# Attention and mixture-of-experts layer on one core: front with the norm in halves, loads in another order, fourth chunk's projections behind the first scores

## Chip, cores and metric

The kernel runs on one core of a Trainium2 chip. The metric is the device time in microseconds of one execution. Before the change three runs gave 443.89 to 449.31, with a median of 449.29.

## Reference

One layer: pre-norm attention with 16 heads of 8 columns, rotary position and a bias by relative distance, then a mixture of 8 experts (top 2 of 8, capacity 512) with a fallback for tokens that found no place. x has 2 batches of 1024 tokens of 128 columns.

```python
h = layernorm(x)
q, k, v = heads(h @ Wq + bq), heads(h @ Wk + bk), heads(h @ Wv + bv)
q = q * cos + rotate_half(q) * sin
k = k * cos + rotate_half(k) * sin
att = (einsum('bhid,bhjd->bhij', q, k) + bias[None]) * (1.0 / sqrt(D))
att = softmax(where(causal, att, -inf))
x = x + merge(einsum('bhij,bhjd->bhid', att, v)) @ Wp + bp
x = x + ffn(layernorm(x))       # router, top 2, experts, fallback
```

## The kernel before

The 2048 tokens are 16 tiles of 128 rows, handled as four chunks (c = 0 to 3) of four tiles; chunks 0 and 1 are batch 0. The 32 pairs of batch and head form 8 groups (n = 0 to 7) of four heads. One list, PLAN, holds all steps in order; each engine walks it and takes the steps that are its own, so the order of an engine's instructions is the order of the list. PROLOGUE is its beginning, called the front here:

- LN: VectorE's statistics of x (L1275, L1279), the reciprocal roots by three Newton steps, and xn_bias (L1283). XN c: the normalised tiles of chunk c (chunk 0 on VectorE, L1288, the others on ScalarE, L836). XT c: TensorE transposes them (L985), ScalarE copies them out (L844).
- VEC and ZERO: VectorE finishes the two vectors of relative-position factors and bias (L1294 to L1297), from which SP writes g_vec and r_vec, and clears ps_av (L1333).
- PROJ c i: q (i = 0) or k (i = 1) of chunk c, four passes of 512 columns (L997, L998), and VectorE's rotation (L1308, L1310, for chunks 0 and 1 also the sum L1317). For chunks 2 and 3 the sum is ADD, on GpSimd (L696).
- HI, REST, MID, LO c i: q and k are split into three bf16 parts: ScalarE rounds (HI, L853), GpSimd subtracts (REST, L702), ScalarE rounds (MID, L863), GpSimd subtracts (LO, L706). Then SP stores the parts (L527) and loads them into q_stack and k_stack in another layout (L565, L572, L575); half_in[0] and half_in[1] count the loads of chunks 0 and 1.
- LOAD: ScalarE issues the loads of b_all and f_all, tables of the other twelve heads, from r_vec and g_vec (L502). SP loads those of the first four heads.

Behind it follow, interleaved by the tables S_BEFORE and M_BEFORE: S n su, a score unit of group n for the row maxima (matmuls L1020 and L1024, VectorE's reduction L1346); M n h, the maxima of half h, turned and written to max_rows (L1152, L1354, L1356), which SP puts into q_stack (L591); ST, a transposed score (L1099), which for the first unit of a half waits for that put, and its exponential on ScalarE (L910); GpSimd's near product (L729, L732); AV (L1128). S, M and PROJ share two PSUM slots in turn, so a step's matmuls wait until VectorE has read the step two places earlier. FLIP turns f_all on TensorE (L1107). VP projects the values (L1004).

keep_warm runs matmuls whose result nobody reads (L964): WARM_FIRST of them before the bias vectors (L971, L975), WARM_PROJ after. GpSimd clears rows of the stacks first, waits for w_in (all four weights), and issues six small DMAs (L682 to L687).

## Time and profile before

| | |
|---|---|
| three runs | 449.29, 449.31, 443.89 us |
| profiled execution, its own time | 449.1 us |
| its span in the profile | 447.6 us |
| TensorE matmul busy | 383.8 us, 86% |
| VectorE busy | 309.2 us, 69% |
| ScalarE busy | 223.9 us, 50% |
| GpSimd busy | 268.4 us, 60% |

Times are from the start of the span. A row of a timeline has the start and the length of an instruction (or of several merged ones, with their number), and in brackets how long its engine was idle before it and who ended that. PE is TensorE, DVE is VectorE, ACT is ScalarE, POOL is GpSimd; SPq and ACTq are the queues from which SP and ScalarE issue DMAs. The granted clock is 1.00 at 2.4 GHz and 0.50 at 1.2 GHz.

### The profile page before, as it was taken

What the parts mean: (1) busy time and instruction counts of PE and PEld (TensorE: products, weight loads), DVE (VectorE), ACT (ScalarE), POOL (GpSimd) and SP (SyncE); (2) the same over time, 40 slices, a digit from 0 to 9 for tenths busy, and PEclk for the clock granted to TensorE, in tenths of its full rate; (3) what the DMA queues carried; (4) which work ended last, traced back from release to release, by engine and by line L of the source; (5) the groups of instructions that cost most, each with busy time, mean ns of one, the idle gap of its engine ahead of it and who ended that gap; (6) DMA issues with size and microseconds to landing.
All of it is one profiled execution on the core that took longest, in us unless ns stands there. A gap on an engine that the chain in (4) does not pass through costs nothing.

```text
span 447.6 us, 7356 instructions
## 1 busy us (share of the span) xinstructions
PE 383.8 (86%) x2470; PEld 177.6 (40%) x2470; DVE 309.2 (69%) x722; ACT 223.9 (50%) x498; POOL 268.4 (60%) x242
## 2 busy tenths in 40 slices
PE   8885788999999999999989989997878677999810
PEld 2432434444434334444435334432334325566500
DVE  3786787866777876877875998875366548566514
ACT  1650245767666776666677755767741110333200
POOL 7375084578569778558589358779712460166650
PEclk9998999999999999999999999999985678999965
DMA  8596574203705008906005000004600102133118
GB/s 217 113 269 155 104 153 79 34 1 80 174 1 101 11 0 185 292 17 109 2 1 103 8 2 9 14 8 130 213 15 13 36 29 57 52 95 95 47 46 277
DMA packets 30459, 37.45 MB, mean 84 GB/s; under 512 B 4757, under 2 KB 25045, under 8 KB 30101
## 3 DMA queue, kind: packets, MB, share of 16 engines
q1 hardware_dynamic: 24378, 29.91, 27.8%
q0 software_dynamic: 2240, 4.21, 3.1%
q10 hardware_dynamic: 3808, 2.92, 2.3%
q8 instruction: 18, 0.29, 0.3%
q14 instruction: 15, 0.12, 0.1%
HBM read 28.56 MB, written 12.75 MB: 92 GB/s over the span
## 4 chain that ended last, share of the span: by engine, by line
PE 62%; DVE 18%; DMA 5%; POOL 5%; ACT 4%; issue 4%; SPq 1%; DVEq 0%; POOLq 0%; ACTq 0%
PE ps_av L1128 15%; PE ps_st L1099 12%; PE ps_slot L1020 12%; DVE neg_max L1346 7%; PE ps_slot L1024 5%; PE ps_st L1203 3%; PE ps_slot L1213 3%; ACT probs L910 2%; PE ps_slot L1159 2%; POOL probs L732 2%; DMA x_sb<-in_L_attn_x_dram 2%; PE ps_st L1205 2%; PE ps_st L1107 2%; PE ps_av L1205 1%; PE ps_st L1041 1%
## 5 line engine op out<-in xcount | busy, mean ns | idle before, releaser
L910 ACT ACTIVATE probs<-ps_st 128x512 f32<-128x512 f32 (+3 forms) x384 | 168.7, 494 | 102.0 <-PE ps_st L1099 99.8
L1346 DVE TENSOR_REDUCE neg_max<-ps_slot 128x1 f32<-128x640 f32 (+7 forms) x184 | 175.6, 989 | 55.0 <-PE ps_slot L1024 52.9
L732 POOL TENSOR_TENSOR probs<-probs,f_all 128x960 f32<-128x960 f32 (+2 forms) x65 | 123.8, 1904 | 10.3 <-ACT probs L910 5.5
L1020 PE MATMUL ps_slot<-k_stack,q_stack 128*128 128x512 bf16 (+3 forms) x384 | 99.5, 329 | 11.3 <-DVE neg_max L1346 6.3
L1099 PE MATMUL ps_st<-q_stack,k_stack 128*128 128x512 bf16 (+3 forms) x384 | 103.1, 329 | 2.8 <-ACT probs L910 2.5
L1128 PE MATMUL ps_av<-probs,v_all 128*9 128x512 f32 (+3 forms) x768 | 81.2, 497 | 2.1 <-POOL probs L732 1.6
L729 POOL TENSOR_SCALAR_AFFINE_SELECT probs<-probs 128x512 f32<-128x512 f32 x58 | 37.0, 638 | 68.7 <-ACT probs L910 68.5
L1024 PE MATMUL ps_slot<-b_all,flip_b 128*128 128x240 bf16 (+2 forms) x288 | 65.4, 252 | 0.0
L1099 PEld LDWEIGHTS ps_st<-q_stack,k_stack 128*128 128x128 bf16 x384 | 34.5, 97 | 74.0 <-ACT probs L910 54.0
L1020 PEld LDWEIGHTS ps_slot<-k_stack,q_stack 128*128 128x128 bf16 x384 | 35.8, 98 | 44.7 <-DVE neg_max L1346 13.1
L737 POOL DMA_INDIRECT slots<-token_rows,slot_no x32 | 33.2, 1039 | 32.3 <-DVEq L1534 24.4
L800 POOL DMA_INDIRECT parts<-probs,e_tok x32 | 31.1, 972 | 31.7 <-DVE probs L1661 23.3
L1024 PEld LDWEIGHTS ps_slot<-b_all,flip_b 128*128 128x128 bf16 x288 | 28.4, 99 | 13.9 <-issue 0.3
L1128 PEld LDWEIGHTS ps_av<-probs,v_all 128*9 128x9 f32 x768 | 11.7, 89 | 25.3 <-issue 18.0
L936 ACT ACTIVATE y_raw<-ps_st 128x512 f32<-128x512 f32 x16 | 9.6, 597 | 23.7 <-PE ps_st L1205 12.9
L1203 PE MATMUL ps_st<-probs 128*128 128x512 f32 x32 | 17.4, 626 | 2.0 <-DVE probs L1623 2.0
L1213 PEld LDWEIGHTS ps_slot<-k_stack,probs 128*128 128x128 f32 x128 | 14.9, 191 | 6.5 <-issue 3.7
L1213 PE MATMUL ps_slot<-k_stack,probs 128*128 (+1 forms) x128 | 16.0, 278 | 1.4 <-DVE probs L1650 1.4
L702 POOL TENSOR_TENSOR token_rows<-token_rows,part_all 128x512 f32<-128x512 f32 x6 | 7.4, 1229 | 13.9 <-ACT part_all L853 13.9
L1159 PE MATMUL ps_slot<-wide,y_raw 128*128 128x128 f32 x64 | 10.7, 292 | 3.8 <-DVE neg_max L1346 3.1
L964 PE MATMUL ps_st<-part_all,ones_b 128*128 128x512 bf16 x34 | 11.6, 444 | 1.6 <-POOL part_all L673 1.6
L930 ACT ACTIVATE probs<-ps_slot 128x512 f32<-128x512 f32 x8 | 4.8, 596 | 16.0 <-PE ps_slot L1195 16.0
(188 smaller groups left out, 403.5 us busy)
## 6 DMA issues: line engine op xcount, KB each, us to landing
q_stack<-q_parts SPq DMA_DIRECT2D x21, 192.0 KB
slots<-in_c_rows_dram SPq DMA_DIRECT2D x4, 528.0 KB, 9.3
probs<-slots SPq DMA_DIRECT2D x8, 264.0 KB, 2.7
parts<-in_c_rows_dram SPq DMA_DIRECT2D x4, 512.0 KB, 9.4
q_stack<-parts SPq DMA_DIRECT2D x4, 512.0 KB, 5.5
k_stack<-k_parts SPq DMA_DIRECT2D x14, 128.0 KB
f_all<-g_vec ACTq DMA_DIRECT2D x1, 1536.0 KB, 11.3
q_parts<-part_all SPq DMA_DIRECT2D x16, 96.0 KB, 3.3
```

Source lines behind the costliest of these rows:

```text
L729: pool.affine_select(out=diag, in_=diag, compare_op=ALU.is_ge, fill=0.0, base=0, pattern=[[0, HG], [1, P]], channel_multiplier=-1).then_in ...
L732: pool.tensor_tensor(pr, pr, f_of[:, n % (H // HG), :, fo:fo + hi - lo], ALU.mult).then_inc(near_done, 1)
L737: pool.indirect_dma_start(slots[:, :], bass.IndirectOffsetOnAxis(ap=slot_no[:, k, t:t + 1], axis=0), u_rows[:, t, :], None, bounds_check=E ...
L800: pool.indirect_dma_start(parts[:, :], bass.IndirectOffsetOnAxis(ap=e_tok[:, i, j:j + 1], axis=0), e_out[i][:, j, :], None, bounds_check=2 ...
L910: act.activation(probs[:, u % PBUF, g, c0:512], ps_st[:, ST_NO[what] % 3, c0:512], ACT.Exp, scale=SCALE).then_inc(exp_done, 1)
L1020: pe.matmul(ps_slot[:, slot, o + lo:o + hi], q_stack[:, buf, t // MT, g, t % MT * P:(t % MT + 1) * P], k_stack[:, buf, lo // CW, g, 0:hi - ...
L1024: mm = pe.matmul(ps_slot[:, slot, o + nlo:o + nhi], flip_b[:, :], b_of[:, n % (H // HG), g, f0:f0 + nhi - nlo], start=False, stop=True)
L1099: pe.matmul(ps_st[:, i % 3, c0:512], k_stack[:, n % NBUF, kt // CH, g, kt % CH * P:(kt % CH + 1) * P], q_stack[:, n % NBUF, qb, g, c0:512] ...
L1128: mm = pe.matmul(ps_av[32 * g:32 * g + VW, c0:512], v_all[:, n, kt, g, :], probs[:, u % PBUF, g, c0:512], start=(u in (0, CH)), stop=(u in ...
L1203: pe.matmul(ps_st[:, c, :], wgu[i][:, c * P:(c + 1) * P], slotT[i], start=True, stop=True)
L1213: mm = pe.matmul(ps_slot[:, 1, i * 512 + j * C:i * 512 + (j + 1) * C], gated[i][:, c, j * P:(j + 1) * P], wd_all[:, bass.ds(2 * e + c, 1), ...
L1346: dve.tensor_reduce(neg_max[:, t // MT, heads[0]:heads[-1] + 1, t % MT], src, AX.X, ALU.max, negate=True).then_inc(slot_used, 1)
```

## The change

LN comes in two halves of eight tiles. The first is whole on VectorE. Of the second, VectorE does the statistics and the first guess of the roots; the three Newton steps and the bias are late_roots on GpSimd, and XN 2 and XN 3, now in pieces of two tiles, wait for it. On SP's queue Wq and Wk stand behind x part 0, the rotary table comes in two halves, and Wv and Wp stand last; the four weights have two semaphores. LOAD waits for half_in[0] too and stands at the end of the front. The first heads' f_all is loaded after the first stacks. The first warming has 16 matmuls, not 24, the second 8, not 10. The steps of chunks 0 and 1 are interleaved in another way, and PROJ and ADD of chunk 3 stand between S 0 6 and M 0 0.

```diff
-WARM_FIRST, WARM_PROJ, WARM_SLOTS = 24, 10, 8
+WARM_FIRST, WARM_PROJ, WARM_SLOTS = 16, 8, 8
...
-    [0, 0, 0, 0, 0, 0, 0, 0, 0, 0, 0, 0, 0, 1, 1, 3, 7, 10, 13, 13, 16, 16, 16],
+    [0, 0, 0, 0, 0, 0, 0, 0, 0, 0, 0, 0, 1, 1, 3, 6, 9, 13, 13, 16, 16, 16, 16],
...
+LAST_CHUNK = [("PROJ", 3, 0), ("PROJ", 3, 1), ("ADD", 3, 0), ("ADD", 3, 1)]
...
             out.append((S_BEFORE[n][su], ("S", n, su)))
+            if (n, su) == (0, M_AT[0]):
+                out += [(0, item) for item in LAST_CHUNK]
...
+            load_x(0)
+            sp.dma_start(w_attn[:, 0, :], Wq[:, :]).then_inc(wqk_in, 16)
+            sp.dma_start(w_attn[:, 1, :], Wk[:, :]).then_inc(wqk_in, 16)
+            load_x(1)
+            load_turns(0)
+            load_x(2)
+            load_x(3)
+            load_turns(1)
+            for i, w in enumerate((Wv, Wp)):
+                sp.dma_start(w_attn[:, 2 + i, :], w[:, :]).then_inc(w_in, 16)
...
-            load_tiles(sp, f_all, g_vec, 0, HG, factors_in)
...
                 load_k(0, 0, (c,), half_in[c])
+            load_tiles(sp, f_all, g_vec, 0, HG, factors_in)
...
-            pool.wait_ge(w_in, 64)
+            pool.wait_ge(w_in, 32)
...
+            def late_roots():
+
+                r = slice(TPB, TT)
+                v, t, dst = newton[:, 0, r], newton[:, 1, r], rstd[:, 0, r]
+                pool.wait_ge(late_guess, 1)
+                for _ in range(3):
+                    after(pool.tensor_tensor(t, dst, dst, ALU.mult))
+                    after(pool.tensor_tensor(t, t, v, ALU.mult))
+                    after(pool.tensor_scalar(t, t, -0.5, 1.5, ALU.mult, ALU.add))
+                    after(pool.tensor_tensor(dst, dst, t, ALU.mult))
+                after(pool.tensor_tensor(xn_bias[:, r], mv[:, r, 0], dst, ALU.mult))
+                after(pool.tensor_scalar(xn_bias[:, r], xn_bias[:, r], -1.0, None, ALU.mult))
+                pool.sem_inc(late_bias, 1)
...
-            act.wait_ge(w_in, 64)
+            act.wait_ge(wqk_in, 32)
...
                     act.wait_ge(vec_out, 32)
+                    act.wait_ge(half_in[0], HALF_IN)
                     load_tiles(act, b_all, r_vec, HG, H - HG, toep_rest)
...
+                if h:
+                    root_guess(rstd[:, 0, r], newton[:, 0, r])
+                    dve.sem_inc(late_guess, 1)
+                else:
+                    rsqrt(rstd[:, 0, r], newton[:, 0, r], newton[:, 1, r])
+                    dve.scalar_tensor_tensor(out=xn_bias[:, r], in0=mv[:, r, 0], scalar=-1.0, in1=rstd[:, 0, r],
+                                             op0=ALU.mult, op1=ALU.mult).then_inc(bias_done, 1)
```

GpSimd's queue in the front, before: the last two of the six DMAs, then REST (L702) and LO (L706) of chunk 0.

```order
L686 DMA fw<-in_L0_ffn_fWu_dram 128x64
L687 DMA fw<-in_L0_ffn_fWd_dram 64x128
L702 ISA
L702 TENSOR_TENSOR token_rows<-token_rows,part_all 128x512 [waits part_hi] x2
L706 TENSOR_TENSOR part_all<-token_rows,part_all 128x512 [waits part_mid] x2
L702 TENSOR_TENSOR token_rows<-token_rows,part_all 128x512 [waits part_lo,part_hi] x2
L706 TENSOR_TENSOR part_all<-token_rows,part_all 128x512 [waits part_mid] x2
```

The same place after. L774 to L779 are late_roots, of whose 14 instructions the last six stand here; REST is L722, LO is L726.

```order
L774 TENSOR_TENSOR newton<-rstd 128x8 [waits own_pool]
L775 TENSOR_TENSOR newton<-newton 128x8 [waits own_pool]
L776 TENSOR_SCALAR newton<-newton 128x8 [waits own_pool]
L777 TENSOR_TENSOR rstd<-rstd,newton 128x8 [waits own_pool]
L778 TENSOR_TENSOR xn_bias<-mv,rstd 128x8 [waits own_pool]
L779 TENSOR_SCALAR xn_bias<-xn_bias 128x8 [waits own_pool]
L722 TENSOR_TENSOR token_rows<-token_rows,part_all 128x512 [waits own_pool,part_hi]
L726 TENSOR_TENSOR part_all<-token_rows,part_all 128x512 [waits part_mid]
L722 TENSOR_TENSOR token_rows<-token_rows,part_all 128x512 [waits part_hi]
L726 TENSOR_TENSOR part_all<-token_rows,part_all 128x512 [waits part_mid]
L722 TENSOR_TENSOR token_rows<-token_rows,part_all 128x512 [waits part_lo,part_hi] x2
L726 TENSOR_TENSOR part_all<-token_rows,part_all 128x512 [waits part_mid] x2
```

The 14 instructions stand between the six DMAs and REST 0 0, and LO 0 0 now stands before REST 0 1.

VectorE's queue at the first score units, before: the end of chunk 3's rotations (L1308, L1310), seven reductions of S (L1346), and the first M (L1354, L1356).

```order
L1308 SCALAR_TENSOR_TENSOR probs<-ps_slot,bcol_perm,wide 128x512 [waits rope_half,slot_full]
L1310 SCALAR_TENSOR_TENSOR probs<-ps_slot,bcol_perm,wide 128x512
L1308 SCALAR_TENSOR_TENSOR probs<-ps_slot,bcol_perm,wide 128x512 [waits rope_half,slot_full]
L1310 SCALAR_TENSOR_TENSOR probs<-ps_slot,bcol_perm,wide 128x512
L1346 TENSOR_REDUCE neg_max<-ps_slot 128x4 [waits rope_half,slot_full]
L1346 TENSOR_REDUCE neg_max<-ps_slot 128x2 [waits slot_full] x6
L1354 CAST max_rows<-ps_slot 16x128 [waits slot_full]
L1356 TENSOR_TENSOR max_rows<-ps_slot,max_rows 16x128 [waits mrows_sb0]
```

After: rotation L1364 and L1366, reduction L1404, M L1412 and L1414.

```order
L1404 TENSOR_REDUCE neg_max<-ps_slot 128x4 [waits rope_half,slot_full]
L1404 TENSOR_REDUCE neg_max<-ps_slot 128x2 [waits slot_full] x6
L1364 SCALAR_TENSOR_TENSOR probs<-ps_slot,bcol_perm,wide 128x512 [waits slot_full]
L1366 SCALAR_TENSOR_TENSOR probs<-ps_slot,bcol_perm,wide 128x512
L1364 SCALAR_TENSOR_TENSOR probs<-ps_slot,bcol_perm,wide 128x512 [waits rope_half,slot_full]
L1366 SCALAR_TENSOR_TENSOR probs<-ps_slot,bcol_perm,wide 128x512
L1412 CAST max_rows<-ps_slot 16x128 [waits rope_half,slot_full]
L1414 TENSOR_TENSOR max_rows<-ps_slot,max_rows 16x128 [waits mrows_sb0]
```

The four instructions of chunk 3's rotations now stand between the seven reductions and the first M.

SP's queue from the store of r_vec to the first stack loads, before:

```order
L547 DMA r_vec<-y_raw 16x384 [waits vec_done]
L547 DMA g_vec<-y_raw 16x384
L502 DMA b_all<-r_vec 128x4x256 [waits vec_out]
L502 DMA f_all<-g_vec 128x4x256
L527 DMA q_parts<-part_all 32x3x512 [waits part_lo]
L527 DMA k_parts<-part_all 32x3x512 [waits part_lo]
L565 DMA q_stack<-q_parts 24x2048 [waits first_out0]
```

And after:

```order
L567 DMA r_vec<-y_raw 16x384 [waits vec_done]
L567 DMA g_vec<-y_raw 16x384
L509 DMA b_all<-r_vec 128x4x256 [waits vec_out]
L547 DMA q_parts<-part_all 32x3x512 [waits part_lo]
L547 DMA k_parts<-part_all 32x3x512 [waits part_lo]
L584 DMA q_stack<-q_parts 24x2048 [waits first_out0]
```

The load of f_all is gone from this place; it stands behind the stack loads of both halves.

## Rows read from the trace of the kernel before

**Rows 1.** Stretches: busy time per engine, granted clock (PEclk), DMA share, GB/s

```profile
40.00:41.00 1.00, 1.00 (x6) 0.63 (x5) 0.43 (x2) 0.00 (x0) 0.00 (x0) 0.50 0.60 184
...
80.00:90.00 10.00, 10.00 (x70) 4.43 (x69) 8.12 (x11) 8.12 (x17) 6.86 (x6) 1.00 0.09 17
```

**Rows 2.** Chain of waits, 0 to 80 us: start, length, what

```profile
27.59 4.97 DMA q_parts<-part_all
...
35.23 2.94 DMA k_stack<-k_parts
...
71.86 0.39 PE ps_st L1099
```

**Rows 3.** Timeline of VectorE: start, length, line, what, idle before

```profile
7.14 1.82 DVE L1275 BATCH_NORM_STATS2 stats<-x_sb 128x6 f32<-128x128 f32 x8 [0.64 <-DMA x_sb<-in_L_attn_x_dram]
...
10.01 0.87 DVE L1275 BATCH_NORM_STATS2 stats<-x_sb 128x6 f32<-128x128 f32 x4 [1.04 <-DMA x_sb<-in_L_attn_x_dram]
...
10.91 1.17 DVE L1279 BATCH_NORM_AGGREGATE mv<-stats 128x2 f32<-128x6 f32 x16
...
14.76 0.17 DVE L1283 SCALAR_TENSOR_TENSOR xn_bias<-mv,rstd 128x16 f32<-128x16 f32 x1
...
15.88 0.54 DVE L1294 TENSOR_TENSOR y_raw<-y_raw,y_all 16x384 f32<-16x384 f32 x1
...
17.13 0.48 DVE L1333 MEMSET ps_av<- 128x512 f32 x1 [0.18 <-DVE bcol_perm L1297]
...
19.38 0.75 DVE L1308 SCALAR_TENSOR_TENSOR token_rows<-ps_slot,bcol_perm,wide 128x512 f32<-128x512 f32 x1 [1.76 <-PE ps_slot L998]
```

**Rows 4.** Timeline of TensorE, warming and bias vectors

```profile
1.59 9.37 PE L964 MATMUL ps_st<-part_all,ones_b 128*128 128x512 bf16 x24 [1.59 <-POOL part_all L673]
...
10.89 1.46 PE L971 MATMUL ps_slot<-y_all,tab 32*16 32x384 f32 x4
...
12.75 2.32 PE L964 MATMUL ps_st<-part_all,ones_b 128*128 128x512 bf16 x10
```

**Rows 5.** Timeline of GpSimd in the front

```profile
11.30 0.74 POOL L682 DMA_DIRECT2D router<-in_L_ffn_Wr_dram  x1 [2.08 <-DMA w_attn<-in_L_attn_Wp_dram]
...
14.59 0.54 POOL L687 DMA_DIRECT2D fw<-in_L_ffn_fWd_dram  x1
...
22.39 1.15 POOL L702 TENSOR_TENSOR token_rows<-token_rows,part_all 128x512 f32<-128x512 f32 x1 [7.26 <-ACT part_all L853]
...
25.95 2.72 POOL L706 TENSOR_TENSOR part_all<-token_rows,part_all 128x512 bf16<-128x512 f32 x2
```

**Rows 6.** Timeline of GpSimd, roots of the second norm, first and last

```profile
223.45 0.22 POOL L753 TENSOR_TENSOR newton<-rstd 128x16 f32<-128x16 f32 x1 [0.66 <-DVEq L1417]
...
227.31 0.24 POOL L760 TENSOR_SCALAR xn_bias<-xn_bias 128x8 f32<-128x8 f32 x1
```

**Rows 7.** Timeline of ScalarE in the front

```profile
21.68 0.63 ACT L853 ACTIVATE part_all<-token_rows 128x512 bf16<-128x512 f32 x1 [1.26 <-DVE token_rows L1317]
...
24.66 1.63 ACT L836 ACTIVATE probs<-x_sb,xn_bias,rstd 128x128 f32<-128x128 f32 x4
```

**Rows 8.** Line L519's issue, then DMA issues with us to landing

```profile
L519 SPq DMA_DIRECT2D wide<-in_c_wide_dram x1: 432/432/432, 5.7 to 5.7; - x1
...
f_all<-g_vec ACTq DMA_DIRECT2D x1, 1536.0 KB, 11.3
...
wide<-in_c_wide_dram SPq DMA_DIRECT2D x1, 1024.0 KB, 9.1
...
r_vec<-y_raw SPq DMA_DIRECT2D x1, 12.0 KB, 2.0
```

**Rows 9.** Timeline of VectorE, last rotations and first maximum

```profile
32.74 0.75 DVE L1308 SCALAR_TENSOR_TENSOR probs<-ps_slot,bcol_perm,wide 128x512 f32<-128x512 f32 x1 [0.64 <-PE ps_slot L998]
...
34.46 0.75 DVE L1308 SCALAR_TENSOR_TENSOR probs<-ps_slot,bcol_perm,wide 128x512 f32<-128x512 f32 x1 [0.31 <-PE ps_slot L998]
...
46.44 0.28 DVE L1354 CAST max_rows<-ps_slot 16x128 bf16<-16x128 f32 x1 [0.37 <-PE ps_slot L1152]
```

More of the change, by code:

```diff
@@ L382, in layer_kernel @@
         t_in = sem("t_in")
-        rope_in = sem("rope_in")
+        rope_in = [sem(f"rope_in{h}") for h in range(2)]
+        bv_in = sem("bv_in")
         ones_in = sem("ones_in")
@@ L831, in _, with normalise @@
             act.activation(below_b[:, :], below, ACT.Copy).then_inc(const_b, 1)
[L833 to L835 removed]
+            def normalise(c, tiles):
+                for t in tiles:
+                    if c < 2:
+                        act.wait_ge(bias_done, 1)
+                    else:
+                        act.wait_ge(late_bias, 1)
                     act.activation(xn[c][:, t % CH, :], x_sb[:, t, :], ACT.Identity, bias=xn_bias[:, t:t + 1],
@@ L872, in _ @@
                 if kind == "XN":
-                    if what[1]:
-                        normalise(what[1])
+                    c = what[1]
+                    if c == 1:
+                        normalise(c, range(CH, 2 * CH))
+                    elif c:
+                        first = c * CH + what[2] * CH // 2
+                        normalise(c, range(first, first + CH // 2))
                 elif kind == "XT":
@@ L1269, in _, with first_norm @@
             stat_count = [0]
-            def first_norm():
-                for t in range(TT):
+            def first_norm(h):
+                tiles = range(h * TPB, (h + 1) * TPB)
+                for t in tiles:
                     if t % CH == 0:
```

57 lines of the change are left out of this document (32 added, 25 removed).

## Prediction

> **What bounds the kernel now.** I read the chain of waits first, then the timeline of 0 to 80 us, the stretches with the granted clock, and the DMA landings. After 80 us TensorE is busy all the time (10.00 of 10 us in the stretch 80:90, VectorE 8.12 [rows 1]), and the diff changes nothing there. So the change can only move the moment from which TensorE runs without gaps. That moment is the first transposed score of group 0's second half, at 71.86 [rows 2].
>
> Ahead of it stand two chains. The first is the front: x lands in four parts, the last statistics start at 10.01, the bias is there at 14.76 + 0.17, the first rotation starts at 19.38 [rows 3]; its split runs through ScalarE and GpSimd, the q part is stored at 27.59 (4.97 us to land), and the last k_stack load (issued 35.23, 2.94 us) lands at 38.17 [rows 2]. Only then does the first score unit run. The second is group 0's maxima on VectorE: seven units, then M at 46.44 [rows 9], and on to 71.86. VectorE has nothing to do in the last 3 us before 38.2: its last rotation starts at 34.46 and takes 1.4 us [rows 9]. A task that now lies in those 3 us is free.
>
> **The norm in halves.** x part 1 now queues behind Wq and Wk (640 KB instead of 512 KB up to its end). Before, it landed at 7.14 and part 3 at 10.01 [rows 3]; I take 8.0. Four statistics 0.87 (8.9), eight aggregates at 1.17/16 = 0.07 us each (9.5), the chain to the bias (14.76 - 12.08 = 2.7) gives 12.2, the first normalise 1.1 gives 13.3. Then VectorE does the second half before the vectors: eight statistics 1.8, eight aggregates 0.6, three steps of the guess 0.6: 16.3. VEC and ZERO took from 15.88 to 17.61 [rows 3], 1.7 us, so the first rotation can start at 18.0. TensorE's side: 24 warming matmuls took 9.37, so 16 end near 7.8; the bias vectors' matmul started at 10.89 [rows 4] at the latest when its inputs were there; 1.86 us more to the second warming, which is now 8 x 0.23 = 1.9. So TensorE is free for x at 14.65 or earlier; transpose, copy and projection took from 15.9 (normalise done, VEC starts) to 19.38, 3.5 us, which gives 18.1 at most. VectorE and TensorE are level: rotation at **18.0 instead of 19.38, 1.4 us earlier**, its sum at 20.3.
>
> **What GpSimd now has in its queue.** Each of its three steps must be passed by REST(0,0). First, it waits for w_in before six DMAs; these took 11.30 to 15.13 [rows 5]. Wv and Wp were ahead of the rotary table, and are now behind it: the bytes on SP's queue up to their end are those up to the table's end before (x, four weights, 1024 KB), and that landed at 5.75 + 9.1 = 14.85 [rows 8]. So the six DMAs run from about 15.2 to 19.0. Second, the roots: 14 small instructions, each waiting for the one before. The same 14 stand in the trace later, from 223.45 to 227.55 [rows 6]: 4.1 us, giving 23.1. Third, REST(0,0), which started at 22.39 before [rows 5]; HI(0,0) would have been ready for it at 20.3 + 0.63 = 20.9. So it starts at **23.1, 0.7 later than before**, and the 1.4 us won on VectorE are not seen. If the weights landed where they did before (11.3), the roots would end at 16.3 + 4.1 = 20.4 and REST would start at 21.0; if at 16.5, at 24.7. I take 14.85, the equal byte count.
>
> From there: REST 1.15 (24.3), MID 0.63 (24.9), HI(0,1) (25.6), REST(0,1) behind LO(0,0) 26.2 to 27.4. In between ScalarE has four tiles of the late norm (1.63 [rows 7]) and a copy like HI's 0.6: MID(0,1) 27.9 to 28.5, LO(0,1) 1.2: the k part is stored at 29.7 (28.70 before).
>
> **The tables later.** ScalarE's 2304 KB for the other heads, which took 11.3 us to land [rows 8], lay over the first stores and loads. Now they wait for half_in[0]. A store with free DMA engines landed in 2.0 (r_vec [rows 8]) against 4.97. So k lands at 31.8; four issues of 0.37 follow, the last load takes between 2.0 and 2.94: first score unit at 35.3 to 36.2, I take 35.8, **2.4 earlier** than 38.2. With the bounds on the weights above it is 33.4 to 37.4. What the tables now lie over: loads for the second half (needed about 12 us later), and the put of the first maxima. 2304 KB and some 1.6 MB on SP's queue from 36 on end by about 48, when the first maxima go out. I count nothing, up to 3 us if that put is late. The first four heads' factors are issued at about 40 and needed at 51: nothing.
>
> At this place the trace gives GpSimd beside VectorE: two L706 in 2.72, 1.36 each, against 1.15 for an L702 [rows 5]. The Trainium skill (SBUF — State Buffer, Who interferes with whom) says more: a GpSimd instruction and a VectorE one with two SBUF inputs exclude each other for their whole duration. By that rule the two sums of rotations at 19 to 23 would put up to 1.4 us on the roots and the time at 451.8. The row doesn't ask for that much, so I leave it out.
>
> **The fourth chunk's projections.** They leave the 3 us in which VectorE waited and go between unit 6 and M(0,0), where VectorE is the chain. A rotation waits for its projection, and two in a row started 34.46 - 32.74 = 1.72 apart [rows 9]. The slot for the first comes free at the end of unit 5; the projection takes 1.72 and some 0.3 until VectorE sees it, less a unit's 1.1 on VectorE (seven from 38.2 to 46.07): 0.9 idle. Then 1.7 and 1.5 for the second: 4.1, less the 0.37 for which M waited before [rows 9]: **3.75 us more**. Between 3.0 (the bare work) and 4.2 (nothing saved). The scores' order in group 0 is put back by one unit: one more after the first AV, one fewer before it; I count zero. The two ADDs on GpSimd (two of about 1.2, as L702) end before its first near product. The new waits for bv_in and w_in stand at the values' projection, after 50 us, and both transfers have landed by 17; ScalarE's copies of Wq and Wk start earlier than before and nobody waits for them.
>
> **Sum.** 449.1 (profiled run) - 2.4 + 3.75 = **450.4**, against a median of 449.29 that the profiled run matches within 0.2. Bounds: -4.8 + 3.0 gives 447.3, -0.8 + 4.2 gives 452.5. A measurement of this kernel tells 2% (9 us) from no change, not this.
>
> **Rivals.** (a) The later gaps of VectorE take up part of the 3.75, or GpSimd is not in the way: first unit at 33.8, 1.5 us added: 446.2. For it: VectorE does wait for TensorE now and then after 46 us. Against: it is the queue in front of TensorE's gaps there. (b) **Slower:** TensorE's clock falls in the new gap. Warming ends at 7.8 and the next matmul waits until 10.1 to 10.9, up to 3.1 us. In the trace TensorE stood from 34.4 to 38.2 and the granted clock was 0.50, 1.2 GHz, at 40:41 [rows 1]. If it falls here, the bias vectors, eight warming matmuls, transposes and first projection take double: 1.9 + 1.9 for the first two and some 2.4 of the 3.5 us more, 5.7 to 6.2 in all, which puts the rotation's sum at 26 and REST(0,0) at 26.6, 3.5 past the 23.1: up to 453.9, half of that if the clock comes back on the way. It decides once the gap is long enough for the clock; shorter gaps than 3.8 us bring no fall in the trace. The Trainium skill (TensorE: Matmul & The Clock Gate, HAM oscillation) says the same of a DMA wait: the next matmuls run at half rate. By that rule this rival holds if this gap is long enough, which no row shows. (c) The late put of the first maxima, 3 us on top: 453.4. (d) The three runs of before spread from 443.89 to 449.31; if the changed kernel's median is of the lower kind, it is 450.4 - 5.4 = 445. (e) The norm in halves does nothing, because x part 1 lands only at 10: rotation at 20.0, still ahead of GpSimd's 23.1, so 450.4 again.
>
> **Chances.** Forecast with (e) 0.55, time 450.4, own range 447.3 to 452.5. (a) 0.15, (b) and (c) 0.13 together, (d) 0.17. The range takes in (d) and (b): 444.5 to 453.8. No case reaches 2% (440.3 or 458.3): same 0.96, 0.02 on each side.
>
> **What the profile would show.** GpSimd's REST(0,0) starting right behind the roots near 23; Wv and Wp landing near 15; k's store landing in about 2 us; first score unit near 35.8; two rotations and some 4 us between unit 6 and M(0,0) at about 47.8; the first transposed score of the second half near 73. Wrong if GpSimd is free by 21, if the clock row of 10 to 14 reads 0.5, or if VectorE's added 3.75 is not found again at 72.

## The result and the profile after

The changed kernel is **slower, by 2.0%**: a median of 456.95 us in four runs (454.50 to 459.26) against 449.06 in four runs of the kernel before, a ratio of 1.0203 with a 95% interval of 1.0109 to 1.0296. So the loss is clear of the noise, and whether it reaches 2% is open. The forecast was 450.4, with a range of 444.5 to 453.8. The profiled execution took 459.26 with a span of 457.2, the longest of its four; before it was 449.1 with 447.6. So the two profiles differ by 10.2 us and the medians by 7.9.

From the first maxima behind 100 us on, the two traces run side by side: the maxima's cast that stands at 103.75 before stands at 111.98 after, 8.2 later, and the last one, at 305.85, stands at 314.08, again 8.2 later. So the time is lost before 80 us. The chain of waits of the changed kernel (start, length, what) names the transfers that end last:

```profile
7.18 9.14 DMA w_attn<-in_L_attn_Wp_dram
...
31.53 1.82 DMA k_parts<-part_all
...
35.15 2.74 DMA q_parts<-part_all
...
43.52 9.13 DMA k_parts<-part_all
...
57.35 9.31 DMA k_parts<-part_all
...
67.93 0.23 PE ps_st L1146
```

The first row is the wait for Wv and Wp. The next two are stores of chunk 0 and of chunk 1 for the first four heads. The last two DMA rows are the stores of group 1 and of groups 2 and 3. Before, the chain had the 4.97 us of q_parts at 27.59 and then none of these stores [rows 2].

**Front.** GpSimd's timeline, the answer to [rows 5] and [rows 6]: it waits 7.40 us for Wp, issues six DMAs, does the 14 small root instructions (L774 to L779), and only then REST 0 0 (L722), 2.62 later than the 22.39 of before:

```profile
16.62 0.74 POOL L702 DMA_DIRECT2D router<-in_L_ffn_Wr_dram  x1 [7.40 <-DMA w_attn<-in_L_attn_Wp_dram]
...
19.92 0.54 POOL L707 DMA_DIRECT2D fw<-in_L_ffn_fWd_dram  x1
20.57 0.21 POOL L774 TENSOR_TENSOR newton<-rstd 128x8 f32<-128x8 f32 x1
...
22.58 0.51 POOL L777 TENSOR_TENSOR rstd<-rstd,newton 128x8 f32<-128x8 f32 x1
...
24.59 0.24 POOL L779 TENSOR_SCALAR xn_bias<-xn_bias 128x8 f32<-128x8 f32 x1
25.01 1.15 POOL L722 TENSOR_TENSOR token_rows<-token_rows,part_all 128x512 f32<-128x512 f32 x1 [0.18 <-POOL xn_bias L779]
```

VectorE in the front and at the first maxima, the answer to [rows 3] and [rows 9]. The rotation starts at 18.39 instead of 19.38; between the last reduction and M stand chunk 3's two rotations, with 1.01 and 0.31 idle ahead of them, and M comes at 49.15 instead of 46.44:

```profile
8.32 0.87 DVE L1324 BATCH_NORM_STATS2 stats<-x_sb 128x6 f32<-128x128 f32 x4 [1.96 <-DMA x_sb<-in_L_attn_x_dram]
9.23 0.64 DVE L1328 BATCH_NORM_AGGREGATE mv<-stats 128x2 f32<-128x6 f32 x8
...
12.32 0.17 DVE L1337 SCALAR_TENSOR_TENSOR xn_bias<-mv,rstd 128x8 f32<-128x8 f32 x1
...
18.39 0.75 DVE L1364 SCALAR_TENSOR_TENSOR token_rows<-ps_slot,bcol_perm,wide 128x512 f32<-128x512 f32 x1
...
45.88 0.75 DVE L1364 SCALAR_TENSOR_TENSOR probs<-ps_slot,bcol_perm,wide 128x512 f32<-128x512 f32 x1 [1.01 <-PE ps_slot L1043]
...
47.60 0.75 DVE L1364 SCALAR_TENSOR_TENSOR probs<-ps_slot,bcol_perm,wide 128x512 f32<-128x512 f32 x1 [0.31 <-PE ps_slot L1043]
...
49.15 0.28 DVE L1412 CAST max_rows<-ps_slot 16x128 bf16<-16x128 f32 x1
```

TensorE, the answer to [rows 4] and further on. It has a gap of 1.96 ahead of the bias vectors; one of 3.84 in which it waits for the late norm (ScalarE's L876, which waits for the roots); the first score unit at 37.75; the wait for the put of the first maxima, their transfer into q_stack (1.12); and at 67.93 a wait of 2.36 for ScalarE. The first transposed score of the second half comes at 79.85, 71.86 before [rows 2]:

```profile
1.60 6.29 PE L1009 MATMUL ps_st<-part_all,ones_b 128*128 128x512 bf16 x16 [1.60 <-POOL part_all L693]
9.84 1.46 PE L1016 MATMUL ps_slot<-y_all,tab 32*16 32x384 f32 x4 [1.96 <-DMA y_all<-in_c_mask_dram]
...
12.04 3.20 PE L1009 MATMUL ps_st<-part_all,ones_b 128*128 128x512 bf16 x8
...
28.17 0.95 PE L1030 MATMUL ps_st<-wide,probs 128*128 128x128 f32 x4 [3.84 <-ACT probs L876]
29.81 2.07 PE L1042 MATMUL ps_slot<-acts,w_attn 128*128 128x512 f32 x2 [0.69 <-ACT acts L884]
...
37.75 0.23 PE L1067 MATMUL ps_slot<-k_stack,q_stack 128*128 128x128 bf16 x1 [1.15 <-DMA k_stack<-k_parts]
...
54.12 0.39 PE L1146 MATMUL ps_st<-q_stack,k_stack 128*128 128x512 bf16 x1 [1.12 <-DMA q_stack<-max_rows]
...
67.93 0.23 PE L1146 MATMUL ps_st<-q_stack,k_stack 128*128 128x128 bf16 x1 [2.36 <-ACT probs L955]
...
79.85 0.38 PE L1146 MATMUL ps_st<-q_stack,k_stack 128*128 128x512 bf16 x1
```

Why ScalarE was late at 67.93 is one row of its timeline. HI 2 0 writes part_all, which the stores of groups 2 and 3 still read, and the exponentials of the last units stand behind it:

```profile
67.08 0.63 ACT L893 ACTIVATE part_all<-y_raw 128x512 bf16<-128x512 f32 x1 [3.18 <-DMA k_parts<-part_all]
```

The same copy in the kernel before:

```profile
60.63 0.63 ACT L853 ACTIVATE part_all<-y_raw 128x512 bf16<-128x512 f32 x1 [0.29 <-DMA k_parts<-part_all]
```

The stretches (length, busy time of PE, PEld, DVE, ACT, POOL, granted clock, DMA share, GB/s) answer to [rows 1]. Behind each of the three gaps of TensorE (1.96, 3.84 and 2.36 us) the granted clock is down, to 0.66, 0.50 and 0.66, with 0.77 and 0.80 in the two stretches after the last; before, it was 1.00 in 66:70, 70:74 and 74:78.

```profile
10.00:14.00 4.00, 4.00 (x13) 1.71 (x12) 3.59 (x20) 0.48 (x1) 0.00 (x0) 0.66 1.19 266
...
30.00:34.00 4.00, 4.00 (x7) 1.83 (x8) 0.38 (x1) 2.70 (x6) 3.65 (x4) 0.50 0.28 76
...
66.00:70.00 4.00, 2.04 (x7) 0.92 (x8) 1.11 (x2) 0.96 (x3) 3.92 (x4) 0.92 0.64 113
70.00:74.00 4.00, 2.83 (x9) 0.78 (x8) 3.54 (x4) 1.97 (x5) 2.74 (x4) 0.66 0.13 20
...
80.00:90.00 10.00, 9.49 (x68) 4.33 (x69) 7.88 (x14) 6.61 (x13) 2.60 (x3) 1.00 0.63 89
```

The DMA issues of the first 80 us (queue, KB each, median us to landing) of the changed kernel:

```profile
f_all<-g_vec ACTq DMA_DIRECT2D x1, 1536.0 KB, 15.5
...
q_parts<-part_all SPq DMA_DIRECT2D x8, 96.0 KB, 5.4
k_parts<-part_all SPq DMA_DIRECT2D x8, 96.0 KB, 8.4
```

and of the kernel before:

```profile
q_parts<-part_all SPq DMA_DIRECT2D x8, 96.0 KB, 3.8
k_parts<-part_all SPq DMA_DIRECT2D x8, 96.0 KB, 4.7
```

So the 10.2 us between the profiled executions are: -0.46 up to the first score unit (38.21 to 37.75), +3.17 from there to M (8.23 to 11.40), **+5.28 from M to the second half's first transposed score** (25.42 to 30.70), +1.6 from there to the end of the span and +0.6 around it. Of the 5.28, 3.74 lie ahead of HI 2 0, which starts 17.93 behind M instead of 14.19. The other 1.54 lie behind it, where the granted clock is down.

### The profile page after: what moved, and what is told of

The parts are those of the page before. It is cut to its first block, busy times and chain, and to the rows that moved or that the text cites. A ratio compares the mean times of both kernels' runs of the same rounds, so it can differ in the third digit from the quotient of the medians.

```text
span 457.2 us, 7288 instructions
## 1 busy us (share of the span) xinstructions
PE 380.3 (83%) x2409; PEld 179.6 (39%) x2460; DVE 309.2 (68%) x725; ACT 224.1 (49%) x498; POOL 271.4 (59%) x256
## 4 chain that ended last, share of the span: by engine, by line
PE 57%; DVE 15%; DMA 8%; POOL 6%; issue 5%; ACT 4%; SPq 4%; DVEq 0%; POOLq 0%; ACTq 0%
PE ps_av L1175 14%; PE ps_st L1146 11%; PE ps_slot L1067 10%; DVE neg_max L1404 5%; DMA k_parts<-part_all 4%; PE ps_slot L1071 4%; ACT probs L955 4%; PE ps_st L1250 3%; PE ps_slot L1260 3%; DMA w_attn<-in_L_attn_Wp_dram 2%; PE ps_slot L1206 2%; PE ps_st L1252 2%; PE ps_av L1252 1%; PE ps_st L1088 1%; PE ps_st L1154 1%
## 5 line engine op out<-in xcount | busy, mean ns | idle before, releaser
L1404 DVE TENSOR_REDUCE neg_max<-ps_slot 128x1 f32<-128x640 f32 (+7 forms) x184 | 175.8, 989 | 56.8 <-PE ps_slot L1071 54.7
L1146 PE MATMUL ps_st<-q_stack,k_stack 128*128 128x512 bf16 (+3 forms) x369 | 99.7, 329 | 6.8 <-ACT probs L955 5.0
L1067 PE MATMUL ps_slot<-k_stack,q_stack 128*128 128x512 bf16 (+3 forms) x366 | 96.0, 330 | 9.6 <-DVE neg_max L1404 5.5
L757 POOL DMA_INDIRECT slots<-token_rows,slot_no x32 | 33.4, 1045 | 33.6 <-DVEq L1592 25.6
L726 POOL TENSOR_TENSOR part_all<-token_rows,part_all 128x512 bf16<-128x512 f32 x8 | 9.3, 1158 | 9.8 <-ACT part_all L903 9.8
L1438 DVE SCALAR_TENSOR_TENSOR probs<-probs,f_all 128x960 f32<-128x960 f32 (+2 forms) x7 | 8.5, 1213 | 5.8 <-ACT probs L955 5.8
## 6 DMA issues: line engine op xcount, KB each, us to landing
slots<-in_c_rows_dram SPq DMA_DIRECT2D x4, 528.0 KB, 10.2
```

Of the source, the lines that this page charges most:

```text
L757: pool.indirect_dma_start(slots[:, :], bass.IndirectOffsetOnAxis(ap=slot_no[:, k, t:t + 1], axis=0), u_rows[:, t, :], None, bounds_check=E ...
L1067: pe.matmul(ps_slot[:, slot, o + lo:o + hi], q_stack[:, buf, t // MT, g, t % MT * P:(t % MT + 1) * P], k_stack[:, buf, lo // CW, g, 0:hi - ...
L1146: pe.matmul(ps_st[:, i % 3, c0:512], k_stack[:, n % NBUF, kt // CH, g, kt % CH * P:(kt % CH + 1) * P], q_stack[:, n % NBUF, qb, g, c0:512] ...
L1404: dve.tensor_reduce(neg_max[:, t // MT, heads[0]:heads[-1] + 1, t % MT], src, AX.X, ALU.max, negate=True).then_inc(slot_used, 1)
```

## The experiments

Twelve kernels. The table has the starts in us that their traces show, in the order of the work, and their times. S is the first score unit, M the first maxima's cast, "second half" the first transposed score of it. The comparisons are with the kernel before on the same chip, for the changed kernel as for the others; HI 2 0 has its wait in brackets.

| kernel | REST 0 0 | S | M | HI 2 0 (waited) | second half | median | ratio, 95% |
|---|---|---|---|---|---|---|---|
| before | 22.39 | 38.21 | 46.44 | 60.63 (0.29) | 71.86 | 449.06 | |
| changed | 25.01 | 37.75 | 49.15 | 67.08 (3.18) | 79.85 | 456.95 | 1.0203 [1.0109, 1.0296] |
| a_tables | 26.24 | 38.91 | 50.31 | 64.77 (1.01) | 76.67 | 453.31 | 1.0101 [1.0046, 1.0156] |
| a_proj | 26.41 | 40.19 | 48.86 | 67.05 (0.67) | 79.22 | 457.47 | 1.0161 [1.0096, 1.0227] |
| a_warm | 25.31 | 37.96 | 49.35 | 66.23 (0.25) | 78.87 | 457.70 | 1.0180 [1.0125, 1.0234] |
| a_pool | 23.84 | 36.02 | 48.78 | 65.06 (1.81) | 76.86 | 460.61 | 1.0260 [1.0207, 1.0314] |
| a_pool2 | 22.88 | 35.30 | 47.96 | 64.55 (1.70) | 76.29 | 456.82 | 1.0159 [1.0100, 1.0217] |
| b_proj | 22.00 | 37.60 | 50.02 | 64.41 (0) | 76.47 | 453.52 | 1.0095 [1.0067, 1.0123] |
| b_tables | 21.82 | 34.52 | 42.36 | 64.90 (3.38) | 75.92 | 452.72 | 1.0072 [1.0034, 1.0109] |
| a_combo | 21.64 | 35.57 | 43.57 | 58.69 (1.67) | 70.61 | 448.58 | 0.9973 [0.9936, 1.0011] |
| a_sp | 24.93 | 37.20 | 48.60 | 62.15 (0) | 86.17 | 465.25 | 1.0385 [1.0330, 1.0440] |
| b_sp | 21.88 | 34.45 | 42.46 | 58.07 (1.71) | 82.25 | 458.15 | 1.0193 [1.0159, 1.0227] |
| c_best | 21.22 | 34.48 | 43.15 | 58.12 (0) | 81.31 | 459.85 | 1.0236 [1.0204, 1.0269] |
| c_split | 21.22 | 34.48 | 43.06 | 58.89 (0) | 71.92 | 448.97 | 0.9957 [0.9922, 0.9991] |

### One part undone in the changed kernel

**a_tables**: the other heads' tables where they were.

```diff
-            ("HI", 0, 0), ("REST", 0, 0), ("PROJ", 0, 1), ("XN", 2, 0), ("MID", 0, 0), ("HI", 0, 1), ("PROJ", 1, 0),
+            ("HI", 0, 0), ("REST", 0, 0), ("PROJ", 0, 1), ("LOAD",), ("XN", 2, 0), ("MID", 0, 0), ("HI", 0, 1), ("PROJ", 1, 0),
...
-            ("XT", 3), ("PROJ", 2, 1), ("LO", 1, 0), ("MID", 1, 1), ("LO", 1, 1), ("ADD", 2, 0), ("LOAD",), ("ADD", 2, 1)]
+            ("XT", 3), ("PROJ", 2, 1), ("LO", 1, 0), ("MID", 1, 1), ("LO", 1, 1), ("ADD", 2, 0), ("ADD", 2, 1)]
...
-                    act.wait_ge(half_in[0], HALF_IN)
```

> The changed kernel, with the other heads' tables loaded as before: ScalarE issues them behind HI 0 0, with no wait for half_in[0]. Theory T (the tables, in flight from 38 us, hold up the stores for the next group, so that the load of stack 1 is issued at 52.7 instead of 48.1, the stores behind it land at 66.7 and ScalarE's HI 2 0 waits 3.2 us for them): the first stores take about 5 us again and the first score unit is at 39 to 41, but the 3.2 us wait of HI 2 0 is gone, first maxima to first transposed score of the second half is back from 30.7 to about 26 us, and the time is 3 to 5 us under the changed kernel's (about 453). Rival P (the chunk 3 projections are the price): the distance from first maxima to that score stays at 30 and the time stays or rises by 2. Rival C (TensorE's clock in the front is the price): no fall of the time either.

The score units start 1.16 later, and yet the second half starts 3.2 earlier and the median is 3.6 lower. The distance from M to the second half falls from 30.70 to 26.36 (25.42 before). The late tables cost more behind the first scores than they give ahead of them. What is left, 453.31 against 449.21 of the kernel before beside it, is 4.1, the price that chunk 3's projections have alone (b_proj, below).

**a_proj**: chunk 3's projections back at the end of the front.

```diff
-            if (n, su) == (0, M_AT[0]):
-                out += [(0, item) for item in LAST_CHUNK]
...
-    out = list(PROLOGUE)
+    out = list(PROLOGUE) + LAST_CHUNK
```

> The changed kernel, with chunk 3's projections and sums back at the end of the front, ahead of the first score unit. My prediction's price for them behind unit 6 was 3.75 us on the first maxima. Theory P: first maxima 2.5 to 3.7 us earlier than 49.15 (with the first score unit 0 to 1 later, as VectorE rotates until about 41 there), time 2.5 to 3.7 lower. Theory T: the stores for the next group are still late behind the tables, so HI 2 0 waits longer by what the maxima win, and the time falls by under 1.5 us.

No change of the time. In this front the old place is not free either: chunk 2's rotations wait 3.33 us for TensorE, which waits for the late norm, so the scores start 2.44 later, and M only 0.3 earlier. HI 2 0 waits 0.67 for its stores and not longer, as the expectation had it, and still starts at 67.05; a_warm, the next run, shows the other way there. What the move costs had to be asked of the front of before (b_proj, below).

**a_warm**: WARM_FIRST and WARM_PROJ at 24 and 10 again.

```diff
-WARM_FIRST, WARM_PROJ, WARM_SLOTS = 16, 8, 8
+WARM_FIRST, WARM_PROJ, WARM_SLOTS = 24, 10, 8
```

> The changed kernel, with 24 and 10 warming matmuls as before. Theory C: the granted clock stays 1.00 from 10 to 14 us (0.66 in the changed kernel), first rotation at 17.9 to 18.1 instead of 18.39; if the clock were the cause of the loss the time would fall by 3 us or more. Theories T and P: GpSimd's roots end at 24.9 all the same and the time stays within 1 us.

The gap at 8 to 10 us is gone and the granted clock there is back at full, as the stretch shows:

```profile
10.00:14.00 4.00, 4.00 (x17) 1.53 (x17) 3.56 (x25) 0.48 (x1) 0.00 (x0) 1.00 1.16 277
```

The rotation starts at 18.78, no earlier than the 18.39 of the changed kernel, and the time is the same. The fall of the clock in the warming was there and cost nothing. The second fall, behind the wait for the norm, stands as in the changed kernel: 0.50 in 30:34.

One row of the table asks for more: HI 2 0 waits only 0.25 for its stores here, not 3.18, and yet the second half starts just 1.0 earlier. The stores are not the only way by which time is lost there. The put of the first maxima, beside the tables too, took from 50.35 to 54.45, and then TensorE ran at the lower clock, so that its four passes of FLIP took 3.41 us (1.88 in the changed kernel and before):

```profile
54.50 0.61 PE L1146 MATMUL ps_st<-q_stack,k_stack 128*128 128x512 bf16 x1 [0.58 <-DMA q_stack<-max_rows]
...
54.90 3.41 PE L1154 MATMUL ps_st<-f_all,wide 128*128 128x512 f32 x4
...
54.00:58.00 4.00, 3.50 (x5) 1.52 (x6) 0.91 (x1) 1.19 (x2) 0.00 (x0) 0.50 0.82 158
```

In a_proj it is the same: the put takes 5.06, TensorE waits 2.27 for it, and the four passes take 3.33. Before, the granted clock was 1.00 in 54:58. Whether the fall of the clock hangs on the tables is not shown.

**a_pool** and **a_pool2**: GpSimd's wait for w_in and the six DMAs later, in a_pool ahead of BP 0 (146 us), in a_pool2, whose edit stands here, at the first score unit.

```diff
-            pool.wait_ge(w_in, 32)
-            pool.dma_start(router[:, :], Wr[:, :]).then_inc(late_in, 16)
...
+            def late_loads():
+
+                pool.wait_ge(w_in, 32)
+                pool.dma_start(router[:, :], Wr[:, :]).then_inc(late_in, 16)
...
             for what in PLAN:
...
+                elif what == ("S", 0, 0):
+                    late_loads()
```

> The changed kernel, with GpSimd's wait for Wv and Wp and its six small DMAs moved out of the front to just before the output bias. The roots then start when VectorE's guess is there (16.4) and end near 20.5 instead of 24.9. If GpSimd's queue held the front: REST 0 0 at 21.4 instead of 25.0, XN 2 at 20.6, TensorE not idle for 3.8 us, k stored at 28 instead of 31.5, first score unit near 34.5 instead of 37.8, and the time about 3 us lower (454) if the delay is passed on. Theory T says that the wait of HI 2 0 for its stores stays, since tables and stores move together. Rival: if the front's gain is eaten by later waits on DMAs, the time stays.

> The changed kernel, with GpSimd's wait for w_in and its six DMAs at the first score unit, where GpSimd stood idle for 8 us in the changed kernel's trace. In the run before this one the same DMAs stood ahead of the output bias; the front was better by 3.0 us at the first transposed score of the second half (76.86 against 79.85), and 3.0 us were lost again where AV waited for GpSimd. Here: the same front, no such wait, time 3 us under the changed kernel's, 453.5 to 455. If the later loss was not these DMAs, it is seen again between 150 and 170 us and the time stays at 460.

With the loads out of the way the roots start at 17.02 instead of 20.57 in a_pool2 (GpSimd now waits for VectorE's guess, not for a weight), REST 0 0 comes 2.13 earlier and the score units 2.45:

```profile
17.02 0.20 POOL L767 TENSOR_TENSOR newton<-rstd 128x8 f32<-128x8 f32 x1 [7.80 <-DVEq L1339]
```

That shows who held the front. The profiled run was 454.5, but the median is 456.82, level with the changed kernel's 456.95 and above the 453.5 to 455 expected; four runs each don't tell how much of the 2.45 reaches the end. In a_pool the place was badly chosen. The six issues take 3.9 us of GpSimd at 146.30 to 150.18, where TensorE has no slack:

```profile
154.39 1.04 PE L1181 MATMUL ps_av<-probs,v_all 128*9 128x256 f32 x8 [2.96 <-POOL probs L745]
```

and the time rises to 460.61.

### One part alone in the kernel before

**b_proj**: only chunk 3's projections behind unit 6.

```diff
-            ("PROJ", 3, 0), ("PROJ", 3, 1), ("ADD", 2, 1), ("ADD", 3, 0), ("ADD", 3, 1)]
+            ("ADD", 2, 1)]
...
+LAST_CHUNK = [("PROJ", 3, 0), ("PROJ", 3, 1), ("ADD", 3, 0), ("ADD", 3, 1)]
...
+            if (n, su) == (0, M_AT[0]):
+                out += [(0, item) for item in LAST_CHUNK]
```

> The kernel before, with only chunk 3's projections and sums moved behind score unit 6 of group 0. My price: first maxima 3.75 us later (50.2), passed on in full, time 449.2 + 3.75 = 453. If later gaps of VectorE take it up: 450 or less. If the front's 3 us of VectorE idle ahead of the first unit were needed for other work, less than 3 us as well.

+4.1 us (453.52 against 449.38 of the kernel before beside it). VectorE's timeline has the pattern that the prediction worked out, 1.0 idle, a rotation, 0.3 idle, a rotation:

```profile
46.75 0.75 DVE L1312 SCALAR_TENSOR_TENSOR probs<-ps_slot,bcol_perm,wide 128x512 f32<-128x512 f32 x1 [1.01 <-PE ps_slot L1002]
...
48.47 0.75 DVE L1312 SCALAR_TENSOR_TENSOR probs<-ps_slot,bcol_perm,wide 128x512 f32<-128x512 f32 x1 [0.31 <-PE ps_slot L1002]
...
50.02 0.28 DVE L1358 CAST max_rows<-ps_slot 16x128 bf16<-16x128 f32 x1
```

From S to M it is 12.42 instead of 8.23, and the 4.2 are still there at the second half (+4.6) and at the end.

**b_tables**: only the tables later, behind half_in[0], and the first heads' f_all behind the stacks.

```diff
-            load_tiles(sp, f_all, g_vec, 0, HG, factors_in)
...
                 load_k(0, 0, (c,), half_in[c])
+            load_tiles(sp, f_all, g_vec, 0, HG, factors_in)
...
+                    act.wait_ge(half_in[0], HALF_IN)
```

and LOAD moved from behind PROJ 0 1 to ahead of the last ADD.

> The kernel before, with only the tables moved: the other heads' behind half_in[0], the first heads' f_all behind the stacks. Theory T: first stores land in about 2 us instead of 5, first score unit near 35 instead of 38.2, first maxima 3 us earlier; but the stores for the next group land about 9 us after their issue, the load of stack 1 is issued at 50 or later, HI 2 0 waits 2 us or more, and the first transposed score of the second half is not earlier than 71.9: time 449 to 453. Rival: if the stores are not held up, the 3 us stay and the time is 446.

The front gains 3.7 us (34.52 instead of 38.21), more than the 3.0 that the prediction gave the faster landing, and all of it is lost again, twice over: the second half starts 4.1 later and the median is 3.3 higher. The two stores in its chain of waits:

```profile
40.54 10.04 DMA k_parts<-part_all
...
55.27 9.21 DMA k_parts<-part_all
```

and the copy that waits for the second:

```profile
64.90 0.63 ACT L853 ACTIVATE part_all<-y_raw 128x512 bf16<-128x512 f32 x1 [3.38 <-DMA k_parts<-part_all]
```

That is the pattern of the changed kernel without any of its other edits. Stack 1 is loaded from 50.60 on, at 48.07 before, and M to second half takes 33.6 instead of 25.4. In between TensorE also stands for 3.28 us, up to 45.60, for the stack load of chunk 1, and its granted clock is 0.50 in 46:50; the changed kernel, whose M comes 6.8 later, has neither. So the two lose by the same stores, but not the same microseconds.

The traced execution took 447.88, the shortest of its ten, though its second half starts 4.1 later than before. It had the clock on its side at the end: 1.00 in 300:350 and 0.90 in 350:400, where the trace of before has 0.86 and 0.83. The start of the second half tells what the front costs; the time of one execution has the clock behind 300 us in it as well.

### The parts that are left, and better places

**a_combo**: the changed kernel with tables as before, GpSimd's loads as in a_pool2, warming 24 and 10, and chunk 3 in the front. What stays of the change: the norm in halves, SP's loads by need, the interleaved steps of chunks 0 and 1, the first heads' f_all behind the stacks. The edit is the diffs of a_tables, a_proj, a_warm and a_pool2 together.

> The changed kernel with four of its parts undone: tables issued behind HI 0 0 as before, GpSimd's six DMAs at the first score unit, 24 and 10 warming matmuls, chunk 3's projections back in the front. What remains is the norm in halves with the late roots on GpSimd, the loads in order of need, the interleaved front, and f_all of the first heads behind the stacks. Theory T with the roots' wait: the chain of the front is then the shorter one, first score unit near 36.5, first maxima near 45, first transposed score of the second half near 71, time 447 to 449, level with or just under the kernel before. If the halves are of no use in themselves (a late XN 2 lets TensorE's clock fall), 450 to 453.

448.58 in ten runs, level with before. The first score unit is 2.64 earlier, the second half 1.25 earlier. In the stretch 30:34 the clock is at 1.00, and the longest wait of TensorE for the norm there is 0.91, so the fall at this place went with that wait. The first heads' f_all behind the stacks stays in this kernel, so by itself it costs nothing that shows.

**a_sp**, **b_sp** and **c_best**: does the slow landing come from the tables, or are the stores slow by themselves? The tables are issued by SP behind the stores of groups 2 and 3, in the changed kernel, in the kernel before, and in the changed kernel with a_pool2's loads, full warming and chunk 3 in the front.

```diff
                 store_parts(c, (2, 3), parts_out[c])
+            load_tiles(sp, b_all, r_vec, HG, H - HG, toep_rest)
+            load_tiles(sp, f_all, g_vec, HG, H - HG, factors_rest)
...
-                    load_tiles(act, b_all, r_vec, HG, H - HG, toep_rest)
-                    load_tiles(act, f_all, g_vec, HG, H - HG, factors_rest)
```

> The changed kernel, but the two loads of the other heads' tables are issued by SyncE behind the stores of groups 2 and 3 (about 57 us), not by ScalarE behind half_in[0] (38 us). Theory (the tables, in flight from 38 to 53 us, hold up the stores of group 1, the put of the first maxima and the stores of groups 2 and 3): the stores of group 1 land in 4 us or less, stack 1 is loaded by 48, the put costs TensorE nothing, ScalarE's copy HI 2 0 waits under 1 us, and the first transposed score of the second half comes at 75 to 76.5 instead of 79.85: 452.5 to 454, with the first score unit still at 37.5 to 38. Rival (the stores are slow by themselves, because four groups' parts go out late together; the tables are only there at the time): stores and copy wait as before, 456 to 457. A second rival: the tables now come too late for the turned factors of the next heads near 75 us, 456 or more.

> The kernel before, but the two loads of the other heads' tables are issued by SyncE behind the stores of groups 2 and 3 (about 55 us) instead of by ScalarE at 21.7. Theory: the first score unit comes at 34.5 to 35.5 as with the tables behind the first loads (3.5 us earlier than before), and nothing is given back afterwards: first transposed score of the second half at 68 to 69.5 (71.86 before), 445.5 to 447. Rival (what is gained at the front is taken back by something else on the way, as it was with the tables behind half_in[0]): 449 to 452.

> The changed front (norm in halves, loads by need) with the four parts of the change that cost time put otherwise: tables issued by SyncE behind the stores of groups 2 and 3, GpSimd's wait and six loads at the first score unit, warming 24 and 10, the fourth chunk's projections in front. If the changed front and the late tables add up, the first score unit comes at 33 to 34.5, the first transposed score of the second half at 66.5 to 69, and the time is 443.5 to 447, under the kernel before. Rival (the tail evens it out, or the load is needed earlier): 448 to 450, as with the tables early.

Up to 60 us nearly all is as the theory has it (HI 2 0 still waits 1.71 in b_sp, and nothing in the two others). In a_sp the same stores go out 1.0 to 2.2 us earlier than in the changed kernel and land in about half of its time; HI 2 0 waits for nothing and starts 4.9 earlier:

```profile
k_parts<-part_all SPq DMA_DIRECT2D x8, 96.0 KB, 4.6
```

So the rival "the stores are slow by themselves" is out. But all three times were far off: the other rival, tables that come too late, holds in full. TensorE stands for 9.57 us in a_sp, 11.06 in b_sp and 9.14 in c_best, ahead of FLIP 2. In a_sp:

```profile
73.35 2.08 PE L1153 MATMUL ps_st<-f_all,wide 128*128 128x512 f32 x2 [9.57 <-DMA f_all<-g_vec]
```

In b_sp the load is the longest piece of the chain:

```profile
53.65 16.51 DMA f_all<-g_vec
```

The factors are wanted at 59 to 64 us in these three, and their 1536 KB took 14.7 to 16.5 to land. So the tables can come too early and too late.

**c_split**: a_combo, but only the factors early; the 768 KB of b_all, wanted after 70 us, go behind the stores of groups 2 and 3.

```diff
-                    load_tiles(act, b_all, r_vec, HG, H - HG, toep_rest)
...
                 store_parts(c, (2, 3), parts_out[c])
+            load_tiles(sp, b_all, r_vec, HG, H - HG, toep_rest)
```

> The changed front with early tables, as in the combination that came out level with the kernel before, but only the factors (1536 KB, needed by 60 us, as the run with both loads at 57 us showed) are loaded early by ScalarE; the 768 KB of b_all, which group 1's score units need after 70 us, are issued by SyncE behind the stores of groups 2 and 3, at 53 us. Theory (what is in flight at the front delays stores and loads in proportion, and what is loaded after its deadline is waited for): first score unit at 34.5 to 35.5 (35.57 with both early), first transposed score of the second half at 69 to 70.6, 446 to 449, level with or just under the kernel before. Rival (b_all lands later than group 1's scores need it, as the factors did): TensorE waits on b_all near 70, 450 to 454. Second rival: the freed bytes change nothing, 448 to 449.5.

448.97 in twelve runs against 450.42 of before beside it, a ratio of 0.9957 whose interval just leaves 1 out. It is the best version here, by less than is worth a claim. Its first score unit is 1.1 earlier than a_combo's; its second half, expected at 69 to 70.6, comes at 71.92, 1.3 later than there. Nobody waits for b_all at 70, so the rival of its lateness is out. One thing that can take the gain back is the granted clock, which before is 1.00 from 46 to 82 us:

```profile
46.00:50.00 4.00, 3.72 (x11) 1.89 (x10) 2.21 (x3) 0.76 (x2) 0.00 (x0) 0.50 0.87 168
```

It is 0.87 in 50:54, 0.76 in 66:70 and 0.81 in 70:74 as well. In a_combo it is 0.60 in 66:70. No run holds the clock up there, so how much of the gain it takes is not shown.

## Why the prediction was wrong, by its steps

**The step that failed is "The tables later": "I count nothing, up to 3 us if that put is late."** The sum of bytes was there (2304 KB of tables and 1.6 MB on SP's queue "end by about 48"), and it counted only who is late when all is done, the put. It named the loads for the second half as needed only 12 us later. It left out the stores that go ahead of them, and that these share the engines with the tables: those of group 1 landed in 9.1 us, which moved the load of stack 1 from 48.07 to 52.66, behind that the stores of groups 2 and 3 left later, took 9.3, and held ScalarE at HI 2 0 for 3.18 with the exponentials behind it. The put itself cost 1.12 in the changed kernel (rival (c), a third of its price), and in a_warm and a_proj it was the put, with the lower clock behind it, that held the same place. By b_tables the edit gains 3.7 ahead of S and costs 8.1 between M and the second half; in time it is +3.3, where the sum had -2.4 for the whole front and nothing behind it. The Trainium skill (DMA: Bandwidth & Descriptors, Queues, rings and completion order) says that each DMA engine takes turns between the queues for which it has work, so that a small store on one queue shares every engine with a large load on another. The trace agrees: the same stores took 8.4 us beside the load and 4.6 without it.

**The insertion of chunk 3** was right in mechanism and nearly in size: forecast 3.75 (3.0 to 4.2), measured 3.17 between S and M in the changed kernel, 4.19 there in b_proj, and 4.1 in b_proj's time. With b_tables' 3.3 the two make 7.4 of the 7.9 us between the medians. That they add up so well is in part luck: in the changed kernel itself, undoing the tables gives back 3.6, undoing the projections nothing (a_proj).

**GpSimd's queue** was right in order and short by 1.9. REST 0 0 did start right behind the roots, at 25.01 (forecast 23.1, upper bound 24.7). 1.5 of it is the landing of Wp: 16.32, where equal bytes gave 14.85. Two issues on SP's queue took 1.35 and 1.29 us, at 4.46 and 5.85, where the seven ahead of them took 0.43 to 0.55 each, so Wp's was issued only at 7.18. The roots took 4.26 for 4.1. The k part was stored at 31.53 instead of 29.7; it landed in 1.82, as said. The first score unit came at 37.75 for 35.8, past the bound of 37.4.

**The norm in halves**: the rotation at 18.39 for 18.0. x part 1 landed by 8.3 (forecast 8.0), the bias came at 12.49 (12.2). Rival (e) is out. What it gives is hidden behind GpSimd, as forecast; freed from that (a_combo) the front is 2.64 earlier, and yet the time is level with before.

**Rival (b)**: the clock did fall, after a gap of 1.96 us, and the eight warming matmuls took 3.20 instead of 1.9. The sentence "shorter gaps than 3.8 us bring no fall in the trace" was not even true of the trace of before. There the longest wait of TensorE between 300 and 340 us is 2.07, and the clock behind it is 0.50:

```profile
332.53 0.67 PE L1041 MATMUL ps_st<-wide,token_rows 128*128 128x128 f32 x4 [2.07 <-DVE token_rows L1422]
...
335.00:340.00 5.00, 4.28 (x29) 2.32 (x30) 2.50 (x24) 0.83 (x2) 0.00 (x0) 0.50 0.02 3
```

The Trainium skill (TensorE: Matmul & The Clock Gate, HAM oscillation) has the matmuls behind a DMA wait run at half rate, and the trace agrees in that. But it tells this of longer waits than the 1.96 us here; where they differ, the measurement decides. The fall cost nothing, since VectorE and then GpSimd were the later ones (a_warm: with no fall the time is the same). The wait of 3.84 for the late norm made a second fall that no step of the prediction had: chunk 2's projection passes, two in 2.07 instead of 1.02.

**The two-input rule** of the Trainium skill (SBUF — State Buffer, Who interferes with whom) was priced at up to 1.4 us on the roots. The trace shows one place that fits it, L777 at 22.58 with 0.51 where its like take 0.20, while VectorE's sum of a rotation ran from 22.33 to 23.02. That is 0.31; to leave the 1.4 out was right.

**Rival (a)** and **(d)** are out: nothing of the 3.75 was absorbed, and no run was below 454.5. The range failed because the one term without a row was given zero and a bound that covered only one of the transfers on that queue.

**Smaller slips.** "After 80 us TensorE is busy all the time" was read from one stretch. It fits the trace of before up to 300 us; from there to 447 TensorE is busy for 108.06 of 147 us at a granted clock of 0.83. The forecast did not suffer by it, since the 8.0 us of 80 us are still 8.2 at the last maxima's cast, but the spread of the times does come from there in part (b_tables). The lower bound of 33.4 for the first score unit should be 33.7 by its own steps, and rival (b)'s 453.9 lies just outside the range that is said to take it in.

What stays open: how much of a_pool2's 2.45 us at the first score unit reaches the end, and why c_split and a_combo, whose scores start 2.6 to 3.7 us before those of the kernel before, end within 0.5% of it; their lower clock between 46 and 74 us is one difference, of unknown weight. Also the 2 us by which the profiled changed kernel is longer behind 80 us were not followed up.

## What to carry to other kernels

When a large load is moved later, list every transfer that will then be in flight beside it, each with the buffer that it frees and the engine that waits for that buffer, and price each at the landing times of the crowded stretch, not of the free one. A load has a window: here, issued at 22 us, it delays the first stores, at 35 to 38 the next ones, and behind 53 its own reader waits 9 to 11 us for it. Splitting it by who needs which part first brought the best ratio here (c_split), but only 0.9957. A filler task is free only while the engine that it fills is idle: moved out of 3 us of idle time into the chain of maxima, two projections cost their full 4.1, and in a front made late by something else the old place was no better. And follow the clock along with the waits: a stretch in which TensorE waits more can cost again in the next one, at a lower clock.
